# One attention kernel, one change: the transposed tiles are moved by sixteen block copies on two queues instead of four strip copies on one

## The reference, cut to what matters

```
qh = split_heads(x @ Wq)          # 8 heads, 2048 x 128
kh, vh = split_heads(ctx @ Wk), split_heads(ctx @ Wv)
sim  = einsum('hid,hjd->hij', qh, kh) * SCALE
mean = sim.mean(-1); sim = (sim - mean) * 1.5 + mean
attn = softmax(sim)
out  = einsum('hij,hjd->hid', attn, vh)
x    = x + merge_heads(out) @ Wout + bout
```

## Time and profile before

| | us |
|---|---|
| median of three runs | 1421.11 |
| profiled execution | 1420.5 |
| its span | 1418.8 |
| PE busy | 1330.4 |
| DVE busy | 1121.2 |
| ACT busy | 901.1 |
| POOL busy | 881.1 |

### The profile page before, as it was taken

The page is one execution under the profiler, slowest core; times in us unless marked ns, Lnnn a source line. Parts: engine busy times, 40 slices in busy tenths (PEclk is TensorE's granted clock), DMA queues, the critical chain, the costliest instruction groups (busy, mean ns, idle before and its releaser), DMA issues.

```text
span 1418.8 us, 20495 instructions
## 1 busy us (share of the span) xinstructions
PE 1330.4 (94%) x7244; PEld 1091.6 (77%) x7244; DVE 1121.2 (79%) x1711; ACT 901.1 (64%) x1325; POOL 881.1 (62%) x535
## 2 busy tenths in 40 slices
PE   3999999988999989999999999999999999994998
PEld 3777887887878767777777777787777778773997
DVE  6779988976811778989898998989898898985454
ACT  3534433224565577877777777777878777676674
POOL 1400011213431199998999989989989989874453
PEclk9999999999999999999999999999999999996899
DMA  9102003124666488887888888878878878787572
GB/s 278 20 9 67 2 18 109 47 76 136 232 178 213 151 229 216 212 208 192 213 210 193 216 192 208 219 179 215 210 197 210 210 175 211 182 201 263 183 243 80
DMA packets 171955, 241.22 MB, mean 170 GB/s; under 512 B 34020, under 2 KB 77414, under 8 KB 171857
## 3 DMA queue, kind: packets, MB, share of 16 engines
q1 hardware_dynamic: 156704, 210.21, 58.1%
q10 hardware_dynamic: 13104, 23.86, 5.0%
q0 software_dynamic: 2048, 5.90, 1.1%
HBM read 64.79 MB, written 41.32 MB: 75 GB/s over the span
## 4 chain that ended last, share of the span: by engine, by line
PE 51%; DVE 15%; ACT 5%; issue 4%; DMA 1%; POOL 0%; SPq 0%; ACTq 0%; DVEq 0%; POOLq 0%
PE xa_S L1476 20%; PE xa_O L1493 12%; DVE xa_mxp L1269 5%; PE xa_Y L1430 5%; PE xa_Y L1505 4%; PE ex_H L1928 3%; PE ex_Y L1940 3%; ACT xa_probs L1649 3%; PE xa_O L1430 3%; DVE xa_tq L1282 3%; DVE xa_mx_nb_rinv L1267 2%; DVE hall L1303 2%; DVE xa_mx_nb_rinv L1272 1%; DMA xa_moved<-xa_tq 0%; DVE xa_mx_nb_rinv L1298 0%
## 5 line engine op out<-in xcount | busy, mean ns | idle before, releaser
L1152 POOL TENSOR_TENSOR xa_pT<-xa_moved,xa_pT 128x1024 fp32r<-128x1024 f32 x246 | 586.1, 2406 | 35.6 <-ACT xa_pT L1643 32.4
L1476 PE MATMUL xa_S<-xa_kT,xa_qT 128*128 128x512 f32 x1536 | 397.6, 408 | 14.7 <-ACT xa_probs L1649 11.7
L1649 ACT ACTIVATE xa_probs<-xa_S,xa_mx_nb_rinv 128x1024 f32<-128x1024 f32 x256 | 286.0, 1118 | 174.6 <-DVE xa_mx_nb_rinv L1272 174.6
L1493 PE MATMUL xa_O<-xa_pT,xa_v 128*128 128x512 f32 x1536 | 375.8, 394 | 2.6 <-DVE xa_pT L1325 2.6
L1476 PEld LDWEIGHTS xa_S<-xa_kT,xa_qT 128*128 128x128 f32 x1536 | 286.3, 190 | 102.4 <-ACT xa_probs L1649 41.5
L1493 PEld LDWEIGHTS xa_O<-xa_pT,xa_v 128*128 128x128 f32 x1536 | 289.3, 189 | 68.0 <-DVE xa_pT L1325 2.9
L1282 DVE STREAM_TRANSPOSE xa_tq<-xa_probs 128x1024 f32<-128x1024 f32 x256 | 316.7, 1237 | 13.6 <-ACT xa_probs L1649 5.9
L1643 ACT ACTIVATE xa_pT<-xa_moved 128x1024 fp32r<-128x1024 f32 x254 | 253.8, 1049 | 4.1 <-DMA xa_moved<-xa_tq 3.9
L1267 DVE TENSOR_REDUCE xa_mx_nb_rinv<-xa_S 128x1 f32<-128x1024 f32 x128 | 155.6, 1215 | 79.8 <-PE xa_S L1476 77.5
L1269 DVE TENSOR_REDUCE xa_mxp<-xa_S 128x1 f32<-128x1024 f32 x128 | 157.5, 1230 | 17.7 <-PE xa_S L1476 17.7
L467 PE MATMUL fw_pp<-fw_hT,fw_wqk 128*128 128x512 f32 x384 | 100.7, 413 | 9.9 <-DVE fw_F L613 8.3
(11 more groups left out here) (228 smaller groups left out, 1812.6 us busy)
## 6 DMA issues: line engine op xcount, KB each, us to landing
xa_moved<-xa_tq SPq DMA_DIRECT2D x508, 256.0 KB, 4.5
heads_k<-ci_outs SPq DMA_DIRECT2D x32, 256.0 KB, 2.0
heads_v<-ci_outs SPq DMA_DIRECT2D x32, 256.0 KB, 2.3
heads_q<-ci_outs SPq DMA_DIRECT2D x32, 256.0 KB, 2.2
xa_chunk<-heads_v ACTq DMA_DIRECT2D x32, 256.0 KB, 3.7
ex_w1s<-in_L_ffn_w_dram SPq DMA_DIRECT2D x8, 1024.0 KB, 6.9
ex_w2s<-in_L_ffn_w_dram SPq DMA_DIRECT2D x8, 1024.0 KB, 10.0
xa_chunk<-heads_q ACTq DMA_DIRECT2D x31, 256.0 KB, 3.5
```

What stands on the lines that cost most here:

```text
L1152: pool.tensor_tensor(quadrants(pT[LO], r), unit_moved(r), quadrants(pT[HI], r).bitcast(F32), ALU.subtract).then_inc(lo_ready, 1)
L1476: last = pe.matmul(S[:, k], qT[a][:, i // GT % 2, q], kT[b][h % 2][:, k * 512:(k + 1) * 512], start=(n == 0), stop=(n == 2))
L1493: last = pe.matmul(O[:], v[a][:, j * P:(j + 1) * P], pT[b][:, r % PRING, k], start=(j == 0 and n == 0), stop=(j == JT - 1 and n == 2))
L1649: act.activation(probs[:, unit % RING], S[:, 2 * u:2 * u + 2].rearrange("p a b -> p (a b)"), ACT.Exp, bias=nb[:, s % 2:s % 2 + 1], scale=S ...
```

## The change

Unit p is moved by 16 DMAs of 64 KB: block b of strip a goes to partitions 32b to 32b+31, so rows keep their order, and v is loaded in plain order. SP issues the eight with b = a and b = a^1; ACT issues the eight with b = a^2 and b = a^3, in slot p+4, two behind each high part and two behind each exponential (`move_two`, new). ACT's first pair of a unit waits for what SP waits for. A semaphore of arrivals counts 256 for a unit instead of 64.

```diff
+AHEAD = 4
-        MOVES = 16 * QUADS
+        MOVES = 16 * QUADS * QUADS
-                    "v": vd[h].rearrange("(b i) j c -> i b (j c)", b=QUADS)[:, :, cols]}[kind]
+                    "v": vd[h].rearrange("p j c -> p (j c)")[:, cols]}[kind]
-        def move(eng, p, a):
+        def move(eng, p, a, b):
-            eng.dma_start(dst[:, a].rearrange("p j n -> p (j n)"),
-                          tq[32 * a:32 * a + 32, g % 2, :, keys].rearrange("p b j m n -> p b (j m n)")) \
+            eng.dma_start(dst[32 * b:32 * b + 32, a].rearrange("p j n -> p (j n)"),
+                          tq[32 * a:32 * a + 32, g % 2, b, keys].rearrange("p j m n -> p (j m n)")) \
# SP
-                for a in range(QUADS):
-                    move(sp, p, a)
+                for d in (0, 1):
+                    for a in (0, 2, 1, 3):
+                        move(sp, p, a, a ^ d)
# ACT
+            def move_two(p, k):
+                g, q = divmod(p, GT)
+                if k == 0:
+                    if p == 0:
+                        act.wait_ge(chunk_lo, FIRST)
+                    act.wait_ge(tr_done, 2 * (GT * g + GT - 1) + q // 2 + 1)
+                    if MRING <= p < SLOTS - 1:
+                        for r in (0, 1):
+                            low_until(act, 2 * (p - MRING) + r)
+                for a in ((1, 3), (0, 2))[k % 2]:
+                    move(act, p, a, a ^ (2 + k // 2))
+                m = s - AHEAD
+                issued = 0 <= m < SLOTS
                 for k in range(2):
                     if 0 <= p + 1 < SLOTS:
                         high_part(2 * p + 2 + k)
+                    if issued:
+                        move_two(m, k)
                 ...
                 for k in range(2):
                     if s < SLOTS:
                         exponential(s, k)
+                    if issued:
+                        move_two(m, 2 + k)
```

## The result

The changed kernel takes 1454.62 us (median of 4 runs, 1452.93 to 1459.44) against 1421.45 for the kernel before (4 runs on the same chip, 1420.5 to 1422.39): ratio 1.0239, 95% interval 1.0213 to 1.0265. It is slower by 33 us, outside the forecast range. The profiled execution took 1452.08 us, its span is 1450.3.

What follows compares the result with a forecast made beforehand. PE was taken as the bound, 99% busy in slots averaging 6.17 us. Steady slots 0, start -0.8 and end +0.5 gave -0.3 us on 1420.5, with 0.6 to the median 1420.8 us; range 1417.3 to 1432.

Steps and rivals of the forecast that it cites:

- the price of an issue: Each block copy's issue on ACT or SP was taken at 0.33 us, with bounds of 0.31 and 2.5 us.
- an argument on patterns: The 0.33 us was taken because the new copies' pattern is plain, like that of the two nearest rows.
- The limit of 0.7 us: In steady slots, ACT issues up to 0.7 us each cost nothing, between the exponentials and behind the added wait.
- the sum: Steady attention slots: the added issues hide under other work on ACT and SP, costing 0 us.
- the four signs of being wrong: Wrong if: an ACT issue over 0.7 us, PE waits for ACT in Y slots, ACT waits for landings, DMA share 1.
- The rival: ACT's issues are slow, competing with SP's, deciding from 0.7 us an issue: 1433 us at 0.75, 1493 at 1.0; chance 0.13.
- The added wait: ACT's first pair waits for POOL's low part three units back; exp0 still starts at 807.86, costing 0 us.
- SP: SP's eight issues take 2.6 us a slot against 3.78 for four old ones, under a 2.0 us wait: 0.
- the rival that they fill up: DMA engines, 83% busy, become the bound if packets take longer; at 30% longer +37 us, 1458; no separate chance given.
- The start: Unit 0 lands earlier and ACT's 3.44 us wait shrinks by 1.6 to 2.7 us: gain 0.8 us.
- The end: Behind the last exponential, pairs and six issues on ACT delay copies and the table load: +0.5 us, between 0 and +3.

Runs made afterwards that it cites:

- experiment 4: Kernel before, plus eight tiny copies a slot issued by ACT from SBUF into DRAM, SP's strips untouched: 1569.53 us, ratio 1.1034.
- experiment 3: Kernel before, plus eight tiny copies (32 rows of 16 B) a slot within SBUF issued by ACT, SP's strips untouched: 1693.77 us, ratio 1.1913.
- experiment 7: Changed kernel with one block copy moved from ACT to SP, so SP issues nine and ACT seven: 1438.13 us, ratio 1.0107.
- experiment 2: Changed kernel with all sixteen block copies issued by SP and none by ACT: 1959.47 us (one run) beside 1422.92.
- experiment 9: Kernel before, plus four tiny SBUF copies a slot on ACT, two behind each exponential, none behind the high parts: 1474.24 us, ratio 1.0374.
- experiment 10: Kernel before, plus four tiny SBUF copies a slot on ACT, two behind each high part, none behind the exponentials: 1436.3 us, ratio 1.0095.
- experiment 1: Kernel before with its four 256 KB strip copies, two of them issued by ACT behind the changed kernel's waits: 1423.08 us, ratio 1.0009.
- 6: Changed kernel with ACT's half of a unit's moves issued one slot later, in slot p+5: 1524.56 us, ratio 1.0725.
- 8: Changed kernel with two block copies moved from ACT to SP, so SP issues ten and ACT six: 1497.26 us, ratio 1.0532.

## Why the prediction was wrong

- **The failed step is the price of an issue with the limit set against it**: "I take 0.33 us, by the two nearest rows", and "0.7 each" free. Measured: 0.61 us on ACT. The rows taken both have a side in DRAM; experiment 4 shows 0.31 there and experiment 3 a minimum of 0.51 for both sizes within SBUF. The right row stood in the same view: the old moves' minimum, 542 ns, was the only one from SBUF to SBUF. It was kept as a bound and not taken, for an argument on patterns that no row bore out.
- **The limit of 0.7 us failed too**, and this is worse, as 0.61 lies below it: with the right price the sum would still have said 0, and of the four signs of being wrong the first, an issue over 0.7 us, didn't come. It asked only whether a pair fits at its own place: between the exponentials it does nearly (1.25 us apart from start to start instead of 1.15). It never added the queue up. Eight issues of 0.61, a load of 0.36 and at least 0.8 us between them make 6.1 us. The mean slot of 6.17 would seem to hold that; the slots without a Y, 5.9 us in the prediction itself, don't. And a queue with nothing left has no cover for an issue that takes 1.4 to 2 us, and the old moves' 2.5 us were a sign that such issues occur. The median slots of experiment 7 show the first part, its ten long slots the second.
- **The rival** named dear issues, and its threshold of 0.7 us kept its chance at 0.13. Its reason, that ACT's issues compete with SP's, is not what makes 0.61 us (experiment 2). It charged the excess of each issue over 0.7 us twice a slot. For experiment 9 (mean 0.94) that gives 2 x 0.24 = 0.48 us, and the run shows 52 us in 120 slots, 0.43. This is partly luck: the same working gives as much for experiment 10 (mean 0.95), which lost 0.12.
- **The added wait**: right that it is cheap (experiment 1).
- **SP**: the 8 x 0.33 = 2.6 us came out as 8 x 0.59 = 4.7, more than the four old ones, but its wait for POOL covered it, as the prediction said: 81.0 of 161.8 us are left.
- **The DMA engines**: the rival that they fill up is wrong. Their share fell from 0.83 to 0.75. The landing of 2.1 us was not foreseen.
- **The start**: the gain of 0.8 us did not come. In the kernel after:

```profile
497.37 1.06 ACT L1643 ACTIVATE xa_pT<-xa_moved 128x1024 fp32r<-128x1024 f32 x1 [2.76 <-DMA xa_moved<-xa_tq]
497.38 1.37 ACTq L1024 DMA_DIRECT2D xa_moved<-xa_tq  x2
498.80 1.06 ACT L1643 ACTIVATE xa_pT<-xa_moved 128x1024 fp32r<-128x1024 f32 x1 [0.37 <-issue]
498.82 1.23 ACTq L1024 DMA_DIRECT2D xa_moved<-xa_tq  x2
500.15 1.11 ACT L1649 ACTIVATE xa_probs<-xa_S,xa_mx_nb_rinv 128x1024 f32<-128x1024 f32 x1 [0.29 <-DVE xa_tq L1282]
```

The unit is there 0.5 us earlier than in the earlier trace rows: SP's eight issues take 4.7 us, not 2.6. The two pairs behind the high parts then use that up: the second ends at 500.05, and the exponential comes at 500.15 instead of 499.79.
- **The end**: +0.5 us forecast, bound +3, some +6 measured. The kernel after, behind the last exponential:

```profile
1276.19 4.58 ACTq L1024 DMA_DIRECT2D xa_moved<-xa_tq  x6
...
1280.82 0.60 ACT L1687 ACTIVATE ex_zt<-xa_S 128x512 f32<-128x512 f32 x1 [3.58 <-issue]
...
1286.11 1.28 ACT L1674 ACT_TABLE_LOAD   x1 [2.32 <-issue]
```

The six issues were counted at 2.0 us and take 4.6, and ACT has nothing to run beside them; the copies, the table load and what follows stand behind. The place was right, the size hung on the same 0.33. No run tested the end by itself; but from the last pair of exponentials to the end of the span it is 178 to 186 us in the changed kernel and in experiments 6, 7 and 8, and 171 to 173 in the kernel before and in experiments 1, 9 and 10, which have no blocks to move there.

What stays open: why an issue of ACT takes 1.4 to 2 us about once in nine slots. In seven of the nine cases an issue of SP is long within 2.5 us of it, which would fit one queue holding up the other, but experiment 2 has long ones with SP alone. Apart from these the pairs are hardly stretched: ACT's issues average 0.62 us against a median of 0.61.

No version beat the kernel before. Experiment 1 equals it; PE is 99% busy in its slots from 600 to 1200 us, so an issue scheme has next to nothing to give there.

## What to carry to other kernels

Price a DMA issue by a row of the same kind (SBUF to SBUF against SBUF to DRAM), not of the same size or queue, and when in doubt by the dearer one. Then add up everything that a queue must do in one period, the issues, the loads and the steps between them, before asking whether each piece fits in its place, and hold the sum against the shortest period, not the mean: here 6.1 us fitted a mean of 6.17 and not the slots of 5.9. Leave some reserve above that for an issue that is long now and then. Cutting copies in four multiplies the issues by four whatever they carry. If work must be put on a busy engine's queue, put it where that engine waits anyway, and keep it from between two instructions that others wait for.

## What the runs showed of the hardware

- An issue within SBUF cost 0.51 us at least and 0.59 to 0.61 in a row, for 512 B and for 64 KB alike; 256 KB strips cost 0.54 at least; with the target in DRAM it cost 0.31 at least.
- While one queue issues 256 KB copies, issues on the other stretch: pairs of tiny copies up to 2.65 us against 1.16, a load 1.32 against 0.33 us. The 256 KB issues stretch themselves, to 0.96 us in the mean in the kernel before. With 64 KB copies on both, medians stayed at 0.59 and 0.61, and ACT's queue had nine issues of 1.45 to 1.96 us in 80 slots.
- Sixteen 64 KB copies keep the DMA engines less busy than four of 256 KB with the same bytes (0.75 at 198 GB/s against 0.83 at 205) and land in 2.1 us instead of 4.5.
- Between two issues in a row on SP's queue stand 0.04 us. Where that queue never stood still, the slot came out as the sum of both: sixteen issues gave 10.2 us against 10.4 measured, ten gave 6.6 against 6.7.
